# The experts' up product of a routed layer on one core, taken as three products of high and low parts

## What is computed

```python
logits = silu(x @ rw1 + rb1) @ rw2 + rb2
k_logits, k_index = top_k(logits, 2)
k_prob = softmax(k_logits)
for e in range(8):
    we = sum(where(k_index == e, k_prob, 0.0), axis=-1)
    h = silu(x @ w1[e] + b1[e]) @ w2[e] + b2[e]
    out = out + we[:, None] * h
```

## Time and profile before

| | us |
|---|---|
| median of 3 runs | 684.16 |
| the profiled execution | 685.29 |
| its span, first to last instruction | 683.6 |
| TensorE busy (matmul) | 588.5 |
| VectorE busy | 507.1 |
| ScalarE busy | 508.8 |
| GpSimd busy | 423.3 |

### The profile page before, as it was taken

One profiled execution on the slowest core, in us unless ns is written; L12 is line 12 of the kernel. 1 busy time (PEld: TensorE's weight loads), 2 busy tenths in 40 slices (PEclk: granted clock), 3 DMA queues, 4 the chain that ended last, 5 costly groups with the idle time before them and its releaser, 6 DMA issues. The chain is left out here.

```text
span 683.6 us, 17706 instructions
## 1 busy us (share of the span) xinstructions
PE 588.5 (86%) x5108; PEld 439.8 (64%) x5108; DVE 507.1 (74%) x1888; ACT 508.8 (74%) x1578; POOL 423.3 (62%) x543
## 2 busy tenths in 40 slices
PE   5667789999899899899989989978798989999950
PEld 4444556666666566566666656655577979999940
DVE  6788988999999999999999999997565312222127
ACT  4157799999999999999989999998643434444434
POOL 2660655747668687686776966855366765554535
PEclk9777999999999999999999999999999999999975
DMA  5996678778787788778868878874525777565538
GB/s 142 308 230 202 198 235 248 228 235 248 214 245 241 213 252 246 228 219 260 249 208 242 252 213 247 243 236 148 189 82 174 236 234 228 198 217 185 176 97 274
DMA packets 173125, 149.03 MB, mean 218 GB/s; under 512 B 16182, under 2 KB 162642, under 8 KB 173030
## 3 DMA queue, kind: packets, MB, share of 16 engines
q1 hardware_dynamic: 168054, 139.33, 67.9%
q0 software_dynamic: 4544, 8.44, 3.7%
q10 hardware_dynamic: 432, 0.14, 0.1%
HBM read 83.71 MB, written 65.05 MB: 218 GB/s over the span
## 5 line engine op out<-in xcount | busy, mean ns | idle before, releaser
L711 ACT ACTIVATE P<-NS,nmax 128x256 f32<-128x256 f32 x512 | 254.2, 504 | 50.5 <-DVE nmax L1312 49.6
L1312 DVE CUSTOM_DVE_ANT_0 NS<-psS,bias 128x256 f32<-128x256 f32 x512 | 185.2, 417 | 2.3 <-PE psS L950 1.6
L968 PE MATMUL psT<-ident,P 128*128 128x128 f32 x1024 | 140.0, 281 | 8.9 <-ACT PT L722 8.8
L1267 DVE COPY stage<-psDist 128x768 f32<-128x768 f32 x125 | 118.1, 945 | 33.9 <-issue 25.2
L722 ACT ACTIVATE PT<-psT 128x512 f32<-128x512 f32 x256 | 136.4, 586 | 0.0
L968 PEld LDWEIGHTS psT<-ident,P 128*128 128x128 f32 x1024 | 118.2, 145 | 24.0 <-issue 9.8
L778 ACT ACTIVATE F<-psS,b1T 128x256 f32<-128x256 f32 x156 | 65.4, 471 | 86.5 <-PE psS L1061 86.5
L609 POOL DMA_INDIRECT results_d<-y,row_u x78 | 76.0, 974 | 56.7 <-DVE y L1458 40.8
L711 ACT ACTIVATION_READ_ACCUMULATOR P<-NS,nmax 128x1 f32 x512 | 100.3, 196 | 0.0
L950 PE MATMUL psS<-Kst,Qst 32*128 32x256 f32 x512 | 65.9, 336 | 34.7 <-DVE nmax L1312 29.9
L1061 PE MATMUL psS<-xT,w 128*128 128x256 f32 x312 | 80.6, 381 | 0.3 <-DMA w<-in_L_ffn_w_dram 0.3
(11 more groups left out here) (254 smaller groups left out, 1044.2 us busy)
## 6 DMA issues: line engine op xcount, KB each, us to landing
dist_d<-stage SPq DMA_DIRECT2D x128, 384.0 KB, 3.0
bias<-dist_d SPq DMA_DIRECT2D x256, 192.0 KB, 3.3
w<-in_L_ffn_w_dram SPq DMA_DIRECT2D x39, 512.0 KB, 3.7
x<-slots_d SPq DMA_DIRECT2D x39, 129.0 KB, 3.0
y<-results_d SPq DMA_DIRECT2D x16, 256.0 KB, 5.0
dist_d<-zeros SPq DMA_DIRECT2D x1, 2048.0 KB, 14.4
out_dram<-y SPq DMA_DIRECT2D x8, 256.0 KB, 3.2
results_d<-y,row_u POOLq DMA_INDIRECT x78, 3.0
```

What stands on the lines that cost most here:

```text
L711: act.activation(P[:, p % 2, h, q, :], NS[:, p % 2, h, q, :], ACT.Exp, scale=-1.0, bias=nmax[:, p % 2, k:k + 1], accum_out=lsum[:, b % 2, ...
L968: mm = pe.transpose(psT[:, h, S * k + 128 * q:S * k + 128 * q + 128], P[:, p % 2, h, q, 128 * k:128 * k + 128], ident[:])
L1267: dve.tensor_copy(stage[:, p % STAGES, :, :, :], bank[:, :, 0:2 * RW].rearrange("p h (q c) -> p h q c", q=2)).then_inc(dist_out, 1)
L1312: dve.tensor_tensor_reduce(NS[:, p % 2, h, q, :], psS[:, h, S * q:S * q + S], bias[:, p, h, q, :], 1.0, 3e38, ALU.add, ALU.min, nmax[:, p ...
```

## The change

The loaded up weights and the turned rows are each split on VectorE into a high part (a copy to a float32r tile) and a low part (the value less the high part, also float32r): `wH`, `wL` of 128x512 and `xH`, `xL` of 128x256, two buffers of each. Each up matmul becomes three that add into the same bank: high by high, high by low rows, low weights by high rows. TensorE waits for the splits (`w_split`, `x_taken`) in place of the load. The down product stays as it is. `split_w(0)` stands ahead of `take_closing(2)`, all others ahead of the `take_x` of their job.

```diff
--- before.py
+++ after.py
@@ -312,7 +312,10 @@
         y1 = t("y1", [128, TT, E])
         y2 = t("y2", [128, TT, E])
         x = t("x", [128, DEEP, EK, ROW])
-        xT = t("xT", [128, 2, ET])
+        wH = t("wH", [128, 2, HID], FR)
+        wL = t("wL", [128, 2, HID], FR)
+        xH = t("xH", [128, 2, ET], FR)
+        xL = t("xL", [128, 2, ET], FR)
         F = t("F", [128, 2, HK, ET])
         y = t("y", [128, HELD, EK, E])
         row_u = t("row_u", [128, JOBS, EK], U32)
@@ -370,6 +373,7 @@
             sm("probs"), sm("weighted"), sm("summed"), sm("gated"), sm("added"), sm("stored"))
         gates_turned, gates_out, gates_wide = sm("gates_turned"), sm("gates_out"), sm("gates_wide")
         x_in = [sm(f"x_in{k}") for k in range(DEEP)]
+        w_split, x_split = sm("w_split"), sm("x_split")
         x_turned, x_taken, rows_known = sm("x_turned"), sm("x_taken"), sm("rows_known")
         up, silu, down, y_rows = sm("up"), sm("silu"), sm("down"), sm("y_rows")
 
@@ -1052,14 +1056,16 @@
 
             def go_up(j, half):
                 if half == 0:
-                    pe.wait_ge(w_in[j % DEEP], arrivals(j))
+                    pe.wait_ge(w_split, 2 * j + 2)
                     pe.wait_ge(x_taken, j + 1)
                 past(pe, silu, 2 * j + half - 1)
                 past(pe, max_done, 4 * STEPS if j == 0 else 0)
                 for n in range(2):
                     at = slice(256 * half + 128 * n, 256 * half + 128 * n + 128)
-                    mm = pe.matmul(psH[:, half, ET * n:ET * n + ET], w[:, j % DEEP, 0, at], xT[:, j % 2, :],
-                                   start=True, stop=True)
+                    dst = psH[:, half, ET * n:ET * n + ET]
+                    pe.matmul(dst, wH[:, j % 2, at], xH[:, j % 2, :], start=True, stop=False)
+                    pe.matmul(dst, wH[:, j % 2, at], xL[:, j % 2, :], start=False, stop=False)
+                    mm = pe.matmul(dst, wL[:, j % 2, at], xH[:, j % 2, :], start=False, stop=True)
                 mm.then_inc(up, 1)
 
             def go_down(j, i):
@@ -1447,7 +1453,18 @@
                 dve.tensor_copy(row_u[:, j, :], x[:, j % DEEP, :, E:ROW].rearrange("p k a -> p (k a)"))\
                     .then_inc(rows_known, 1)
                 past(dve, up, 2 * (j - 1))
-                dve.tensor_copy(xT[:, j % 2, :], psX[:, 0:ET]).then_inc(x_taken, 1)
+                dve.tensor_copy(xH[:, j % 2, :], psX[:, 0:ET]).then_inc(x_split, 1)
+                dve.wait_ge(x_split, j + 1)
+                dve.tensor_tensor(xL[:, j % 2, :], psX[:, 0:ET], xH[:, j % 2, :].bitcast(FP), ALU.subtract)\
+                    .then_inc(x_taken, 1)
+
+            def split_w(j):
+                dve.wait_ge(w_in[j % DEEP], arrivals(j))
+                past(dve, up, 2 * (j - 1))
+                dve.tensor_copy(wH[:, j % 2, :], w[:, j % DEEP, 0, :]).then_inc(w_split, 1)
+                dve.wait_ge(w_split, 2 * j + 1)
+                dve.tensor_tensor(wL[:, j % 2, :], w[:, j % DEEP, 0, :], wH[:, j % 2, :].bitcast(FP), ALU.subtract)\
+                    .then_inc(w_split, 1)
 
             def take_rows(j):
                 if j == 0:
@@ -1462,6 +1479,7 @@
                 for n in range(first, last):
                     j, half = n // 2, n % 2
                     if half == 0 and j + 1 < JOBS:
+                        split_w(j + 1)
                         take_x(j + 1)
                     if half == 1 and j > 0:
                         take_rows(j - 1)
@@ -1547,6 +1565,7 @@
             context(B - 1)
             take_x(0)
             take_closing_extra(1)
+            split_w(0)
             take_closing(2)
             take_closing(3)
             tiles(0, 1)
```

## The result

The changed kernel takes 687.13 us (median of 5 runs, 686.59 to 688.86) against 684.16 for the kernel before: ratio 1.0058, 95% interval 1.0035 to 1.008. It is slower, by 2.97 us; the forecast was 681.2. The same kernel, run once more beside other runs of the kernel before, gave 1.0042 (1.0017 to 1.0067).

A forecast was written before the change was run, and what follows sets the result against it. TensorE's own pace was taken to bound the late jobs, other engines now and then the earlier ones; terms summed to -3.0 us, taking the profiled 685.29 to 682.3, or 681.2 against the median; range 677.0 to 688.0.

The forecast's parts named there:

- jobs 0 to 3: While the last tokens are routed: VectorE's chain of choices holds TensorE, four splits are added; +2.1 us.
- plan: Plan of the remaining jobs, between two VectorE row copies: two splits land in a chain without pause; +2.9 us.
- jobs 8 to 15 (-0.8 and +1.8): Jobs 8 and 9 gain 0.8 us; job 15's start loses 1.8, its split following weights that SP's queue issues late.
- jobs 15 to 38: Late steady jobs: 24 jobs gain 0.395 us each from TensorE's shorter job; -9.5 us.
- shared port: VectorE's new cast meeting GpSimd's scatter: 0.5 us early plus 24 x 0.05 in steady jobs; +1.7 us.
- third rival: VectorE's cast meets GpSimd's scatter in every job, up to 0.45 us more each: 687.9 us, slower; chance 0.18.
- Four splits add 6.1 us; idle are 4.75: Jobs 0 to 3: added VectorE work set against its idle time, less some 0.75 of register reads; +2.1 us.
- 24 x 0.395 = -9.5: Late jobs: TensorE's job falls from 3.73 to 3.34 us at 0.1115 a product, VectorE ready at 3.35.
- each excess showing at half: Steady jobs: x us of VectorE time beyond the used-up cover makes the pace 3.34 + x/2.
- Enough, by 0.6: Weight loads in steady jobs: wanted by the cast 4.3 us after issue, against a median landing of 3.7.
- second rival: VectorE's weight cast runs no faster per element than the subtraction, 0.68 us: 685.6 us, no change; chance 0.13.
- fourth rival: TensorE's products do not cost half but 0.22 us each: about 732 us, +51 over the forecast; chance 0.04.

## Why the prediction was wrong

| step | forecast | changed kernel |
|---|---|---|
| jobs 0 to 3 | +2.1 | +4.7 |
| jobs 3 to 5 (to job 6's start) | -1.2 | -0.7 |
| plan (job 6 to job 8) | +2.9 | +3.0 |
| jobs 8 to 15 (-0.8 and +1.8) | +1.0 | +0.7 |
| jobs 15 to 38 | -9.5 | -5.5 to job 38's start |
| shared port | +1.7 | three casts blocked, 0.6 in all |
| sum | -3.0 | +2.3 at job 38, +0.4 behind it |

The value 687.13 lies in the range, by luck: the range reached so far up for the third rival's cause, which did not come. The sign was wrong. Two steps failed, and a third held only in part.

**"Four splits add 6.1 us; idle are 4.75"** set the splits' sum against VectorE's idle time of a window. That idle time does not lie where job 3's split stands: ahead of `h2T`, for which TensorE waits. The splits of jobs 1 to 3 passed 2.8 to 3.3 us on to TensorE in every trace with this order (waits of 3.5 to 4.0 for 0.69). What the prediction didn't have at all is the clock: in the earlier trace rows it is 1.00 throughout, and behind the longer wait TensorE ran at half speed, 1.6 us more. Its share can be seen apart: with the wait at 2.0 us, job 3 was late by 2.7 where the clock fell and by 1.5 where it did not.

**"24 x 0.395 = -9.5"** rests on 0.1115 us a product and on VectorE ready at 3.35. The products stand 0.1185 apart, so that TensorE's own job is 3.43 and not 3.34. The 0.1115 was the down product's, of another type; the prediction's own reading of float32r, 0.12 from the earlier trace rows, was the better price and gives 3.44. VectorE's work was priced right: from `y`'s start to `xL`'s end it took 2.35 us, against 0.84 + 1.53. But `y` came up to 1.15 behind the up product's start instead of 0.94, with the longer register reads, and the handing over to TensorE took 0.10 instead of 0.04: behind a job that started on time VectorE was ready at 3.47 to 3.53. By the prediction's rule, each excess showing at half, that makes 3.45 to 3.48; measured are 3.50, with one job of 3.85. So the rule fits, and the prediction even allowed 0.05 a job, under the port. The size that was off most is the product: 0.09 a job, 2 us over the late jobs. Over 23 jobs both make 3.7 us, 2.5 more than was allowed; the early jobs made 2.6.

**"Enough, by 0.6"**, for the weights' landing, held in most late jobs and not in all. In the changed kernel's first trace one cast of 22 waited for its weights, in the second three, whose jobs took 3.80 to 4.21; with the register read first at least six. The median landing hid the tail: the earlier trace rows has 6.2 as the longest.

**What was right.** The plan: +3.0 for +2.9, and moving it gave 3.4 to 3.8 us back at job 8. The wait for job 15's weights, the split of 2.1 us behind them, and SP's fills. The cast of the weights at 0.42 to 0.43, near the lower bound of the earlier trace rows: the second rival, 0.68, is out. The products at little over half: the fourth rival is out. The Trainium skill (TensorE: Matmul & The Clock Gate, Part 3: Packing small matmuls) has a weight load overlap matmuls in flight only where the row group differs, beside a word on a background weight buffer; these traces are against the first as it stands, with load and product of the full array in 0.12 us.

**The third rival** gave 687.9, close to what was measured, by another cause: the cast blocked by GpSimd in every job, 0.45 more. That came about in three jobs of 39 of the changed kernel's trace, with casts of 0.59 to 0.61 us instead of 0.42; the mean of the late jobs is 427 ns, and the pace fell to 3.43 with the scatters where they were.

When a cast is blocked can be read from all traces of this study, which hold 426 casts of weights. The 36 that began 0.53 to 0.76 us after a scatter all ended 1.18 to 1.24 us after its start and took 0.46 to 0.70, as if each did its 0.42 from some 0.8 us on; casts that began beside a scatter earlier or later mostly took their 0.42. The small cast of the earlier trace rows, begun 0.54 after its scatter and ended with it, fits. The Trainium skill (SBUF — State Buffer, Who interferes with whom) has, for a cast in a two-port mode beside GpSimd, the one that comes second fully blocked for the whole instruction of the first. In these traces the second waits, but only for that last part of a scatter: a cast that began 0.3 us after one took 0.43 (567.01, above). In the other direction the scatter rose from 972 to 1065 ns, the first of each job's two, which begins during the subtraction of the weights; what lengthens it no run shows, and no one waits for it.

## What to carry to other kernels

Idle time of an engine covers new work only where the work stands in its list; ask for each added instruction which waiting instruction comes behind it and who waits for that one. Where a faster engine lands exactly on the next one's loop, look in that loop for latency that needn't be in it (here a register read behind a wait, 0.64 us a job). And in a chain that already has waits, take the work in only where there is room: plain products in the first ten jobs, or the splits placed by hand, each with the register read ahead and SP's fills spread, made the same change 1.4 to 1.5% faster than the kernel before (give or take 0.6%), some 0.4% of it by the fills alone.

## What was not expected of the hardware

TensorE's granted clock fell to 0.5 behind the longer waits of the routing: in all six traces with a wait of 3.5 to 4.0 us ahead of the ranking matmul, in one of three with a wait of 2.0, and in none of the five with 0.69. About the wait for the next choices, 1.9 to 2.7 us in all kernels, it fell in nine of the fourteen traces: in the first of the changed kernel (528.4 to 532.0), and in four of the five with plain early jobs. The windows of the kernel before with fills spread:

```profile
520.00:524.00 4.00, 3.07 (x10) 2.80 (x11) 1.99 (x12) 0.00 (x0) 1.00 (x2) 0.59 0.12 41
524.00:528.00 4.00, 4.00 (x18) 3.48 (x17) 0.48 (x2) 1.03 (x3) 2.87 (x3) 0.55 0.33 78
```

Job 8 was late by 3.2 us there. That the waits bring the fall about is what these traces suggest, and the length of the wait alone does not decide it: with 2.5 us it fell in some and not in others. The trace of before, on which the prediction rests and from which all lateness here is told, is the one of five with plain early jobs in which it did not happen. In the other four, job 8 was late by 1.1 to 3.2 us with all up products until then plain; as much of the lateness at job 8 in any one trace can be the clock. And products of 256 columns of float32r stand 0.116 to 0.121 us apart, where the eight instructions of a half down product take 0.89.
